# Feed-forward: twelve tiles normalised and added inside its last six blocks and taken first by the router; the projection's statistics issued one tile later

## What is computed

```python
attn_out = _mhsa(h, edge_bias, src, dst, Wq, Wk, Wv, Wp, bp)
h1 = layer_norm(h + attn_out, ln1_g, ln1_b)
ffn_out = gelu(h1 @ W1 + b1) @ W2 + b2
x = x + layer_norm(h1 + ffn_out, ln2_g, ln2_b)
logits = layernorm(x) @ router_w.T
```

## Time and profile before

| | us |
|---|---|
| median of 3 runs | 2792.26 (2792.14 to 2793.42) |
| the profiled execution | 2789.74 |
| its span | 2787.7 |

### The profile page before, as it was taken

The page is one execution under the profiler, slowest core; times in us unless marked ns, Lnnn a source line. Parts: engine busy times, 40 slices in busy tenths (PEclk is TensorE's granted clock), DMA queues, the critical chain, the costliest instruction groups (busy, mean ns, idle before and its releaser), DMA issues. The chain is left out here.

```text
span 2787.7 us, 50123 instructions
## 1 busy us (share of the span) xinstructions
PE 2289.8 (82%) x10903; PEld 1803.5 (65%) x10904; DVE 1490.0 (53%) x2999; ACT 1246.7 (45%) x2511; POOL 716.6 (26%) x720
## 2 busy tenths in 40 slices
PE   1688876889989895997468399995999954999995
PEld 0344443666666663886456288884888853888884
DVE  7799975898888887332733644544002153111113
ACT  1799943777777772223223122343324431222221
POOL 0000011777777770000374311000110006002013
PEclk9999997999999998999589699997999956999998
DMA  5421222777777770000166322221222105656555
GB/s 196 200 76 73 76 82 81 208 212 213 212 212 212 213 203 20 22 0 4 49 212 193 109 76 70 69 67 53 67 67 74 55 2 189 218 191 221 189 204 178
DMA packets 183896, 353.28 MB, mean 127 GB/s; under 512 B 55346, under 2 KB 138727, under 8 KB 179111
## 3 DMA queue, kind: packets, MB, share of 16 engines
q1 hardware_dynamic: 138328, 206.94, 22.9%
q0 software_dynamic: 45520, 145.80, 18.1%
HBM read 275.32 MB, written 77.31 MB: 126 GB/s over the span
## 5 line engine op out<-in xcount | busy, mean ns | idle before, releaser
L2279 PE MATMUL gnn_p<-gnn_y,gnn_counts_wide 128*128 (+1 forms) x2500 | 553.6, 381 | 2.7 <-DVE R_kept L2161 2.6
L2279 PEld LDWEIGHTS gnn_p<-gnn_y,gnn_counts_wide 128*128 128x128 f32 x2500 | 473.1, 191 | 69.1 <-DVE R_kept L2161 6.6
L856 POOL DMA_INDIRECT kv_pair<-kv,gather_idx x448 | 428.1, 956 | 150.6 <-issue 103.6
L2084 ACT CAST gnn_counts_wide<-gnn_counts 128x1664 f32<-128x1664 uint16 x100 | 158.0, 1580 | 387.1 <-PE gnn_p L2279 368.0
L956 PE MATMUL p_edge_q<-QX_kept,onehot_turned 128*128 x904 | 264.1, 415 | 61.6 <-ACT onehot_turned L919 54.7
L1926 ACT ACTIVATE experts_hidden<-experts_p_hidden,experts_pack 128x256 f32<-128x256 f32 x290 | 134.1, 472 | 337.3 <-PE experts_p_hidden L1958 337.3
L1958 PE MATMUL experts_p_hidden<-experts_turned,experts_pack 128*128 128x256 f32 x1160 | 263.6, 383 | 2.1 <-DVE experts_turned L1857 1.2
L956 PEld LDWEIGHTS p_edge_q<-QX_kept,onehot_turned 128*128 128x128 f32 x904 | 155.4, 191 | 166.6 <-issue 151.1
L1967 PE MATMUL experts_p_y<-experts_pack,experts_hidden 128*128 128x256 f32 x1160 | 260.2, 379 | 0.0
L1958 PEld LDWEIGHTS experts_p_hidden<-experts_turned,experts_pack 128*128 128x128 f32 x1160 | 222.7, 192 | 33.6 <-issue 2.8
L964 PE MATMUL p_sums<-R_kept 128*128 128x264 f32 x896 | 237.3, 388 | 0.0
(11 more groups left out here) (376 smaller groups left out, 3214.2 us busy)
## 6 DMA issues: line engine op xcount, KB each, us to landing
experts_pack<-experts SPq DMA_DIRECT2D x29, 2052.0 KB, 8.8
gnn_counts<-adj SPq DMA_DIRECT2D x400, 104.0 KB, 2.2
adj<-adj_counts SPq DMA_DIRECT2D x100, 208.0 KB, 1.9
experts_rows<-slots_in SPq DMA_DIRECT2D x60, 256.0 KB, 3.8
slots_out<-experts_y SPq DMA_DIRECT2D x58, 256.0 KB, 7.7
experts_rest<-experts SPq DMA_DIRECT2D x60, 130.0 KB, 8.0
kv_pair<-kv,gather_idx POOLq DMA_INDIRECT x448, 3.8
slots_in<-R_kept SPq DMA_DIRECT2D x2, 3328.0 KB, 13.9
```

The lines of the kernel that those rows point to most:

```text
L856: pool.indirect_dma_start(kv[r][:, j, :], None, a["kv"], bass.IndirectOffsetOnAxis(ap=idx[r][:, j:j + 1], axis=0)).then_inc(kv_in[r], 16)
L2084: act.copy(wide[b][:], raw[r][:].rearrange("p q s -> p (q s)")).then_inc(wide_ready, 1)
L2279: mm = pe.matmul(bank[:, off:off + D], wide[b][:, j * P:(j + 1) * P], y[:, at(n), :].squeeze(1), start=first and off == 0, stop=last and ( ...
```

## The change

In the projection, the `bn_stats` of tile n - 1 is issued between `part` and `R` of tile n; the last tile's is issued after the loop.

In the feed-forward, the gain and bias rows of the second normalisation (`ln2`) are loaded behind the weights, POOL adds the bias row to all of `X` in five instructions of five tiles, and the first twelve tiles are finished inside the block: after step 5 DVE makes their variance, ACT the square root after its step 6, DVE the factors; then `add_early` comes after each of DVE's steps 7 to 12, for two tiles each time. After the feed-forward only tiles 12 to 24 are left, in chunks of 5, 4 and 4. PE no longer waits for tiles 0 to 11; ACT copies four of them after each chunk's normalisation.

```diff
@@ attention_out, DVE
                 dve.scalar_tensor_tensor(out=part[b][:].unsqueeze(1), in0=X[:, at(n), :], scalar=column(k["RSTD"], n),
                                          in1=pO[b][:, 0:D].unsqueeze(1), op0=ALU.mult,
                                          op1=ALU.add).then_inc(part_ready, 1)
+                if not first or b:
+                    spread_of(n - 1)
                 dve.wait_ge(part_ready, n + 1)
                 dve.scalar_tensor_tensor(out=R[:, at(n), :], in0=part[b][:].unsqueeze(1), scalar=column(k["NMR"], n),
                                          in1=bp[:].unsqueeze(1), op0=ALU.add, op1=ALU.add).then_inc(r_ready, 1)
+
+            def spread_of(n):
                 dve.wait_ge(r_ready, n + 1)
                 dve.bn_stats(ST[:, at(n), :], R[:, at(n), :])
...
             over_tiles(dve, step)
+            spread_of(NT - 1)
@@ ffn_blocks
+    HALF = (BLOCKS - 1) // 2
+    EARLY = BR * HALF
...
             sp.dma_start(pack[:], a["ffn"][0]).then_inc(pack_in, 16)
+            sp.dma_start(ln2[:], a["rows0"][:, 3:5, :]).then_inc(ln2_in, 16)
+
+        @block.gpsimd
+        def _(pool):
+            pool.wait_ge(ln2_in, 16)
+            for lo in range(0, NT, 5):
+                pool.tensor_tensor(X[:, lo:lo + 5, :], X[:, lo:lo + 5, :], ln2[:, 1:2, :].to_broadcast([P, 5, D]),
+                                   ALU.add).then_inc(ln2_added, 1)
...
+            def early_variance():
+                msum, diff, m2, sq = (small[:, c, :] for c in range(4))
+                st = ST[:, 0:EARLY, :]
+                dve.wait_ge(spread, EARLY)
+                link(dve.tensor_tensor(msum, st[:, :, 1], st[:, :, 4], ALU.add))
...
+            def early_factors():
+                rstd = k["RSTD"][:, 0:EARLY]
+                dve.wait_ge(std_ready, 1)
+                link(dve.reciprocal(rstd, small[:, 4, :]))
...
+            def add_early(p):
+                tiles = at(BR * p, BR)
+                for r in range(BR):
+                    tile = R[:, at(BR * p + r), :]
+                    normalise(dve, k, tile, tile, BR * p + r).then_inc(early_normed, 1)
+                dve.wait_ge(early_normed, BR * p + BR)
+                dve.tensor_tensor(R[:, tiles, :], R[:, tiles, :], ln2[:, 0:1, :].to_broadcast([P, BR, D]),
+                                  ALU.mult).then_inc(early_scaled, 1)
+                dve.wait_ge(early_scaled, p + 1)
+                dve.tensor_tensor(X[:, tiles, :], X[:, tiles, :], R[:, tiles, :], ALU.add).then_inc(early_x, 1)
+                dve.wait_ge(early_x, p + 1)
+                for r in range(BR):
+                    dve.bn_stats(ST[:, at(BR * p + r), :], X[:, at(BR * p + r), :])
...
-            over_tiles(dve, step, BLOCKS)
+            step(0, 0, 0, True, False)
+            step(1, 1, 0, True, False)
+            with dve.Fori(1, HALF // 2) as i:
+                step(2 * i, 0, i, False, False)
+                step(2 * i + 1, 1, i, False, False)
+            early_variance()
+            step(HALF, 0, HALF // 2, False, False)
+            early_factors()
+            dve.wait_ge(ln2_added, NT // 5)
+            with dve.Fori(HALF // 2, HALF - 1) as i:
+                step(2 * i + 1, 1, i, False, False)
+                add_early(2 * i - HALF)
+                step(2 * i + 2, 0, i + 1, False, False)
+                add_early(2 * i - HALF + 1)
+            step(BLOCKS - 2, 1, HALF - 1, False, False)
+            add_early(HALF - 2)
+            step(BLOCKS - 1, 0, HALF, False, True)
+            add_early(HALF - 1)
...
+            act.wait_ge(var_ready, 1)
+            act.activation(small[:, 4, :], k["VAR"][:, 0:EARLY], ACT.Sqrt, bias=k["EPSC"][:, 0:1]).then_inc(std_ready, 1)
@@ ffn
-        chunks_ = [(c, slice(lo, hi)) for c, (lo, hi) in enumerate(((0, 6), (6, 12), (12, 17), (17, 22), (22, NT)))]
+        chunks_ = [(c, slice(lo, hi)) for c, (lo, hi) in enumerate(((early, 17), (17, 21), (21, NT)))]
...
-            sp.dma_start(gb[:], a["rows0"][:, 3:5, :]).then_inc(gb_in, 16)
             logits.sync(sp)
...
-                if c:
-                    logits.scalar(act, chunks_[c - 1][1])
-            logits.scalar(act, chunks_[-1][1])
+                logits.scalar(act, slice(4 * c, 4 * c + 4))
+            for _, part in chunks_:
+                logits.scalar(act, part)
             logits.finish(act)
-
-        @block.gpsimd
-        def _(pool):
-            pool.wait_ge(gb_in, 16)
-            for c, part in chunks_:
-                pool.tensor_tensor(X[:, part, :], X[:, part, :], gb[:, 1:2, :].to_broadcast(wide(part)),
-                                   ALU.add).then_inc(b_added, 1)
```

More of the change, by code:

```diff
@@ L1183, in _, with ffn_blocks @@
             over_tiles(pe, step)
-def ffn_blocks(k):
-    nc, a, C, R, ST = k["nc"], k["a"], k["C"], k["R"], k["ST"]
+def ffn_blocks(k, ln2):
+    nc, a, C, X, R, ST = k["nc"], k["a"], k["C"], k["X"], k["R"], k["ST"]
     ident = C[:, C_IDENT:C_IDENT + P]
@@ L1222, in ffn_blocks @@
         y_ready, fin, norm, scaled = sem("_y_ready"), sem("_finish"), sem("_norm"), sem("_scaled")
+        small = sb("_ln_small", [P, 5, EARLY])
+        small_step, spread, var_ready, std_ready = sem("_small_step"), sem("_spread"), sem("_var"), sem("_std")
+        ln2_in, ln2_added = sem("_ln2_in"), sem("_ln2_added")
+        early_normed, early_scaled, early_x = sem("_early_normed"), sem("_early_scaled"), sem("_early_x")
         block = s.enter_context(nc.Block())
@@ L1263, in step @@
                 for r in range(BR):
-                    dve.bn_stats(ST[:, at(BR * j + r), :], R[:, at(BR * j + r), :])
+                    dve.bn_stats(ST[:, at(BR * j + r), :], R[:, at(BR * j + r), :]).then_inc(spread, 1)
+            def early_variance():
[3 more added lines that the diff above has]
+                link(dve.tensor_tensor(msum, st[:, :, 1], st[:, :, 4], ALU.add))
+                link(dve.tensor_tensor(diff, st[:, :, 1], st[:, :, 4], ALU.subtract))
+                link(dve.tensor_tensor(m2, st[:, :, 2], st[:, :, 5], ALU.add))
+                link(dve.tensor_tensor(sq, diff, diff, ALU.mult))
+                link(dve.tensor_scalar(m2, m2, 1.0 / D, None, ALU.mult))
+                dve.scalar_tensor_tensor(out=k["VAR"][:, 0:EARLY], in0=sq, scalar=0.25, in1=m2, op0=ALU.mult,
+                                         op1=ALU.add).then_inc(var_ready, 1)
+            def early_factors():
+                rstd = k["RSTD"][:, 0:EARLY]
+                dve.wait_ge(std_ready, 1)
+                link(dve.reciprocal(rstd, small[:, 4, :]))
+                link(dve.scalar_tensor_tensor(out=k["NMR"][:, 0:EARLY], in0=small[:, 0, :], scalar=-0.5, in1=rstd,
+                                              op0=ALU.mult, op1=ALU.mult))
+            def add_early(p):
[11 more added lines that the diff above has]
+                    dve.bn_stats(ST[:, at(BR * p + r), :], X[:, at(BR * p + r), :])
+            link = Chain(dve, small_step)
             dve.wait_ge(gb_in, 16)
@@ L1282, in _ @@
             act.activation(y[0][:, 0, 0:1], k["EPSC"][:], ACT.Gelu)
-            over_tiles(act, step, BLOCKS)
+            step(0, 0, 0, True, False)
+            step(1, 1, 0, True, False)
+            with act.Fori(1, HALF // 2) as i:
+                step(2 * i, 0, i, False, False)
+                step(2 * i + 1, 1, i, False, False)
+            step(HALF, 0, HALF // 2, False, False)
+            act.wait_ge(var_ready, 1)
+            act.activation(small[:, 4, :], k["VAR"][:, 0:EARLY], ACT.Sqrt, bias=k["EPSC"][:, 0:1]).then_inc(std_ready, 1)
+            with act.Fori(HALF // 2, HALF - 1) as i:
+                step(2 * i + 1, 1, i, False, False)
+                step(2 * i + 2, 0, i + 1, False, False)
+            step(BLOCKS - 2, 1, HALF - 1, False, False)
+            step(BLOCKS - 1, 0, HALF, False, True)
         @block.tensor
@@ L1436, in _ @@
             link = Chain(dve, step_done)
-            dve.wait_ge(gb_in, 16)
             for c, part in chunks_:
                 dve.wait_ge(normed, c + 1)
-                link(dve.tensor_tensor(R[:, part, :], R[:, part, :], gb[:, 0:1, :].to_broadcast(wide(part)), ALU.mult))
-                dve.wait_ge(b_added, c + 1)
+                link(dve.tensor_tensor(R[:, part, :], R[:, part, :],
+                                       ln2[:, 0:1, :].to_broadcast([P, part.stop - part.start, D]), ALU.mult))
                 dve.tensor_tensor(X[:, part, :], X[:, part, :], R[:, part, :], ALU.add).then_inc(x_ready, 1)
```

14 lines of the change are left out of this document (6 added, 8 removed).

## The result

The changed kernel takes **2772.56 us** (median of 3 runs, 2768.87 to 2774.73) against 2792.26; the ratio is 0.9928, with a 95% interval from 0.9904 to 0.9952. The forecast was 2773.0. The profiled execution takes 2772.56 us in place of 2789.74, its span 2770.8 in place of 2787.7. The page's first part shows the same work as before: 2289.7 us of PE against 2289.8, and of POOL's 5 us less, 4 are its five additions, which take 14.87 us in place of 18.83.

A forecast was written before the change was run, and what follows sets the result against it. DVE was fullest in the projection, PE bound the feed-forward, a chain of waits held the router stage. Terms -12.2 + 0.3 + 0.2 + 3.0 + 3.0 - 13.5 = -19.2 us off the 2792.26 median gave 2773.0 us, range 2768 to 2782.

The forecast's parts named there:

- projection: Projection loop: DVE's new order takes a tile from 2.06 to 1.50 us, -12.2 us in all, bounds -13.0 to -5.7.
- added transfer, POOL, variance and factors: Feed-forward: 256 KB more on SP's queue +0.3 us, POOL's additions +0.2, early variance and factors 0.
- four stalls: Feed-forward: add_early after steps 7 to 10 makes PE wait 0.74 us each, +3.0 us, bounds 4 x 0.4 and 4 x 1.5.
- tail: End of feed-forward: the sixth add_early, after the last step with nothing beside it, +3.0 us, bounds 2.8 and 4.
- router stage: After the feed-forward: PE turns tile 0 once router weights and short products are done, -13.5 us, bounds -12 and -14.5.
- Rival 1: Projection: loop register work and waits on counted semaphores pace DVE at 1.8 us a tile, total 2779.6 us; 15%.
- floor that I gave PE: Projection: PE's chain from division to product, with hand-over, allows no tile below 1.50 us; DVE alone 1.47.
- room of 2.3 us: Feed-forward: DVE's slack between the end of prepare and PE's turning of those rows, 2.35 us less 0.06 hand-over.
- Rival 2: Last feed-forward blocks: DVE sets the pace, add_early takes 4.1 us, four stalls of 1.8, total 2778.4 us; 12%.
- rival 5: Feed-forward: PE's clock falls to 1.2 GHz in the new pauses, five blocks double, total 2844 us; 2%.
- Rival 3: Router stage: PE's clock rises as it no longer pauses 12 us ahead of its tiles, total 2765 us; 4%.
- Rival 4: Projection: new order does nothing, tile stays at 2.06 us, and DVE paces the last blocks, total 2790.7 us; 4%.

The follow-up runs named there:

- its repeat: The changed kernel run again unchanged, on a chip where the kernel before takes 3167 us: ratio 0.9948, stretch from projection to raw logits 289.96 us.
- the last experiment: Changed kernel with POOL's five additions held back until DVE has written R of block 0, beside DVE's second burst: one run, 2780.3 us.

## Why the prediction came out right

The time is 0.4 us from the forecast, and the stretch, -19.12, is 0.1 from the sum of -19.2. Both are in part luck. The terms were off by more, to both sides. And 0.4 us is less than executions of one kernel differ (2768.87 to 2774.73): the profiled one took 2772.56 where about 2770.5 was forecast, and on the other kind of chip the same kernel's ratio is 0.9948, where 19.2 us less would be 0.9939.

| term | forecast | measured |
|---|---|---|
| projection | -12.2 | -10.7 |
| added transfer, POOL, variance and factors | +0.5 | -0.3 |
| four stalls | +3.0 | +4.0 |
| tail | +3.0 | +2.9 |
| router stage | -13.5 | -15.0 |

- **Projection.** The mechanism was right: no instruction follows its producer, two of the four steps are as forecast in every tile and the other two in every second tile. The mis-sized term is the loop edge, which I took as covered, together with the waits on registers. Two tiles have two steps of 0.50 us where 0.38 and 0.34 would do; written out, the tile is 1.47. Rival 1 holds to a third: 0.10 of its 0.30 us a tile. The floor that I gave PE, 1.50 us, was 0.03 too high. I had asked that DVE never wait for the product. It does wait, in every tile of the written-out loop, and can: from a division to the end of the product that it releases are 1.78 us (1330.62 to 1332.40), `part` follows 0.05 later, and the division after that `part` 1.11 later (1333.56), which is 2.94 us for two tiles, 1.47 each. DVE's four steps alone would give 1.46, so the two bounds are too close to tell apart. About 0.6 us of the 10.7 lie in the two tiles ahead of the loop (5.87 us before, 5.31 after), which the same code needs 5.87 us for in its repeat. The Trainium skill (Advanced Engine Details and Errata, Engine Queue Depths) has a queue of eight for VectorE, by which I had said that the edge would vanish. It didn't, and the measurement decides.
- **Transfer and POOL.** Free, both. POOL started as its rows landed and DVE was hit once, 3.26 in place of 0.69 us, inside its room. The place and time are as forecast, by a margin of 0.4 us (1123.63 against 1124.05). What I under-rated is how much hung on them: the last experiment puts a price of 9 us on the collision that I had bounded at 1.5. The error was to count only DVE's two-input additions and only one POOL instruction. The Trainium skill (SBUF — State Buffer, SBUF: two separate sides) has the exclusive lock for two-input operations and for those that use both ports for one tensor, and lets a normalisation be among the latter; 5.41 us for two of them agrees, and the 0.75 of the statistics shows one kind that is spared. Whether the normalisations do use both ports isn't shown: alone one lasts 0.41 us, as long as the two-input division of the same size.
- **Stalls.** The room of 2.3 us and the 3.03 of `add_early` (measured 3.08) gave pauses of 0.74; they are 0.86, 0.89, 0.87 and 0.74, 3.36 in place of 2.96. The rest of the miss is that a pause costs more than its length: the four steps grew by 4.25 us in all, some 0.2 each beyond the pauses (the piece as a whole by 4.00). Rival 2 (pauses of 1.8) was wrong, as was rival 5: the clock stays at 1.00 through pauses below 1 us. Its mechanism is real, as the pause of 7.35 us shows.
- **Tail.** 2.88 us, as forecast.
- **Router stage.** The chain that I named was the one; the first turning comes 5.06 us after `finish_ln` starts, 1.1 earlier than forecast, since the router weights land 1.56 us after their issue when nothing is queued ahead of them. The tiles take 31.44 us against 31.8: a hold by ACT for four tiles costs 0.7, not 0.8, which is 0.2 of the difference. Rival 3 did not come about, the clock stays at 1.2 GHz for all 25 tiles, but its condition wasn't met either. The wait of 12 us ahead of the first turning is gone, yet PE stands for 9.68 us ahead of the router product, and its clock is at 0.50 before the first turning. The prediction had overlooked that wait.
- **Rival 4** (the new order does nothing) fell with the tile of 1.60 us.
- **What the prediction missed** is that its second part is two changes. POOL's move earns the gain; the six early pairs, placed where they are, lose 1.8 us, while the same instructions some 5 us later cost nothing, which is worth 7 us. My own rows had it: DVE busy 57.96 of 172 us, most of the rest being its wait for the product in front of which I never asked to place them.

## What to carry to other kernels

When work is moved under a full engine, place it by the feeder's waits: the same DVE instructions cost 1.1 us a block behind the wait for PE's product and nothing in front of it. Before moving an operation that runs beside another engine, ask what that other engine was waiting for, and try moving only that: here POOL's additions alone brought the whole net gain. And give long POOL instructions a stretch in which DVE has nothing due, since each addition or normalisation of DVE that meets one can wait for all of it; `bn_stats` didn't.

## What the runs showed of the hardware that I had not expected

- Two fp32 normalisations on DVE (one SBUF tensor and two columns in, SBUF out) beside POOL's additions lasted 5.41 us in place of 0.72, as blocked as the two-input additions (3.25 in place of 0.69), while `bn_stats` kept its 0.75. In the kernel before, six `bn_stats` from 1327.81 on, beside a POOL addition that ran from 1326.12 to 1330.53, lasted 0.41 to 0.43 each.
- A pause of 0.86 us on PE lengthened the block step by 1.09: the turning after it lasted 0.66 in place of 0.60, and where the rest comes from is open.
- In a pause of 7.35 us PE's granted clock fell: on average 0.77 over 6 us inside the pause and 0.66 over the 6 us that hold its end, and it was 1.00 again from 1142 on. Pauses of 0.9 us every 15 us left it at 1.00.
- On the router's tiles (turnings, and products of 8 columns) PE was busy for 29.29 us of 30 and its clock stayed at 1.2 GHz all the same. It had fallen before them: in the changed kernel PE had stood for 9.68 us ahead of the router product (first row), in the kernel before for 8.11 and then 11.47. No run shows these tiles begun at 2.4 GHz.

```profile
1304.00:1309.00 5.00, 0.47 (x3) 0.47 (x3) 1.52 (x9) 3.61 (x7) 0.00 (x0) 0.50 0.02 2
1310.00:1340.00 30.00, 29.29 (x146) 28.09 (x145) 12.02 (x19) 12.80 (x33) 0.00 (x0) 0.50 0.00 1
```

- A loop edge costs DVE about 0.12 us a turn, and the step with 0.50 in place of 0.34 some 0.16 more, in the tiles where DVE reaches its wait for the product before the product has ended: `part` then follows the product's end by 0.18 us, written out by 0.04 to 0.06. I put that down to a wait on a register's value; all that was shown is that writing the loop out takes both away, 1.60 to 1.47 us a tile.
